# Edge ranks of a graph layer on one core: two TensorE products instead of three, the third term added on GpSimd

## The reference, cut to what matters

```python
def _spmm(row, col, val, x):                     # 53125 edges, sorted by dst
    return jax.ops.segment_sum(val[:, None] * x[col], row, num_segments=3125)
xn = _layernorm(x, axis=-1)
h = _spmm(edge_row, edge_col, edge_val, xn)      # and again in each layer
...
q, k, v = xn @ wq.T, xn @ wk.T, xn @ wv.T        # k and v are layer-normed per head
kv = einsum('bhsd,bhse->bhde', k, v) / S
```

## Time and profile before

| what | us |
|---|---|
| median of 3 runs | 1109.56 |
| their range | 1108.05 to 1111.23 |
| the profiled execution | 1103.93 |
| its span, first to last instruction | 1102.2 |
| records of the 25 tiles, first `spread` to last `kept` | 15.69 to 196.22 |
| busy in the span: PE, DVE, ACT, POOL | 1057.2, 710.7, 327.0, 181.0 |

### The profile page before, as it was taken

How to read it: one execution, slowest core, us unless ns; L and a number is a source line. 1 busy time by engine, 2 the same in 40 slices (tenths; PEclk the granted TensorE clock), 3 DMA queues, 4 the chain that set the end, 5 groups by cost and what they waited for, 6 DMA issues and landing times.

```text
span 1102.2 us, 15231 instructions
## 1 busy us (share of the span) xinstructions
PE 1057.2 (96%) x5391; PEld 662.0 (60%) x5391; DVE 710.7 (64%) x1611; ACT 327.0 (30%) x1067; POOL 181.0 (16%) x218
## 2 busy tenths in 40 slices
PE   4899999999999999999999999999999899999995
PEld 3566666566665665656784444644459466666664
DVE  8999999997766866869840111227777554444444
ACT  4878888312222222222211111211112221212210
POOL 2123444301101010110000000000444611111111
PEclk9999999999999999999999999999999999999998
DMA  6120011123333333423259988897994686555510
GB/s 179 19 58 13 38 48 48 49 96 135 134 135 134 135 134 135 182 101 139 97 220 361 377 300 310 337 334 285 305 325 169 188 238 141 137 136 135 132 38 8
DMA packets 80986, 178.58 MB, mean 162 GB/s; under 512 B 35678, under 2 KB 64122, under 8 KB 68750
## 3 DMA queue, kind: packets, MB, share of 16 engines
q1 hardware_dynamic: 67592, 123.39, 34.9%
q10 hardware_dynamic: 9190, 46.12, 10.6%
q0 software_dynamic: 4128, 8.08, 2.1%
HBM read 116.23 MB, written 63.77 MB: 163 GB/s over the span
## 4 chain that ended last, share of the span: by engine, by line
PE 84%; DVE 10%; issue 2%; ACT 2%; DMA 1%; POOLq 0%; DVEq 0%; ACTq 0%
PE ps L1692 23%; PE ps L1846 20%; PE ps L1971 10%; PE ps L1959 10%; PE ps L1676 8%; PE ps L1651 2%; PE ps L1715 2%; PE ps L1637 2%; PE ps L1671 1%; PE ps L1583 1%; PE ps L1658 1%; DVE W L1119 1%; DVE bst L1232 1%; DMA XX<-in_x 1%; DVE XT L1483 1%
## 5 line engine op out<-in xcount | busy, mean ns | idle before, releaser
L1692 PE MATMUL ps<-RING,XX 128*128 128x512 f32 (+2 forms) x700 | 296.1, 548 | 1.2 <-DVE W L1190 1.2
L1846 PE MATMUL ps<-RING,RY 128*128 128x512 f32 (+4 forms) x750 | 268.6, 514 | 0.1
L1846 PEld LDWEIGHTS ps<-RING,RY 128*128 128x128 f32 x750 | 133.5, 190 | 118.7 <-issue 111.2
L858 ACT COPY RING<-ps 128x512 f32<-128x512 f32 (+3 forms) x163 | 92.6, 568 | 274.9 <-PE ps L1676 258.9
L1692 PEld LDWEIGHTS ps<-RING,XX 128*128 128x128 f32 x700 | 117.5, 190 | 68.4 <-issue 61.6
L1183 DVE TENSOR_TENSOR RING<-RING,RY 128x1536 bf16<-128x1536 bf16 (+1 forms) x150 | 139.9, 939 | 4.0
L1676 PEld LDWEIGHTS ps<-RING 128*128 128x128 bf16 x1575 | 100.6, 97 | 52.0 <-issue 46.4
L1173 DVE TENSOR_TENSOR RING<-iota_p,RY 128x1024 bf16<-128x1024 bf16 (+1 forms) x150 | 96.3, 648 | 29.1 <-PE ps L1676 26.5
L1676 PE MATMUL ps<-RING 128*128 128x128 bf16 (+1 forms) x1575 | 112.9, 217 | 0.0
L995 ACT ACTIVATE RY<-ps,b1T 128x489 f32<-128x489 f32 x64 | 42.9, 671 | 164.8 <-PE ps L1959 164.8
L1550 DVE SCALAR_TENSOR_TENSOR W<-ps,RING,W 128x256 f32<-128x256 f32 (+1 forms) x32 | 15.4, 483 | 90.7 <-PE ps L1971 89.5
(11 more groups left out here) (287 smaller groups left out, 1332.6 us busy)
## 6 DMA issues: line engine op xcount, KB each, us to landing
RING<-adj_dram SPq DMA_DIRECT2D x60, 1280.0 KB, 7.0
adj_dram<-RING ACTq DMA_DIRECT2D x30, 1280.0 KB, 4.6
rbuf_dram<-W SPq DMA_DIRECT2D x8, 516.0 KB, 5.4
RING<-rbuf_dram SPq DMA_DIRECT2D x8, 516.0 KB, 4.0
xbuf_dram<-W SPq DMA_DIRECT2D x8, 512.0 KB, 3.3
XT<-in_L_ffn_w SPq DMA_DIRECT2D x16, 256.0 KB, 5.3
XT<-in_L_ffn_w SPq DMA_DIRECT2D x4, 1024.0 KB, 9.7
RING<-in_L_ffn_w SPq DMA_DIRECT2D x16, 256.0 KB, 5.0
```

Of the source, the lines that this page charges most:

```text
L858: nc.scalar.copy(RING[:, n % 2, at:at + w], ps[:, u % 2, 0:w]).then_inc(s_bev, 1)
L1692: last = nc.tensor.matmul(ps[:, ACC + dd, 0:w], XN[:, j, dd * H:(dd + 1) * H], at[:, i * w:(i + 1) * w], start=(j == 0), stop=True, skip_g ...
L1846: last = nc.tensor.matmul(o, (Y if l == 0 else S0)[:, j, :], RING[:, slot_of[g % 5], i * across + first:i * across + first + w], start=(j ...
```

## The change

- `ranks(j)` has two products in place of three. The first is as before; the second is the identity in fp16 times a new tile `tagged`.
- `tagged` (128 x 468, fp16, two buffers) is made by one addition on POOL: `ohp`, read back in the order of `scan`, plus `scan`. PE waits for it ahead of the second product (`s_tagged`).
- So that `ohp` carries the mark, `paired(j)` multiplies by 1024 while it copies; `kept(j)` multiplies by 1/1024 while it stores the records.
- On ACT `paired(it)` moves to the head of its round, ahead of `weigh(it - 3)`, `cast` and `normal`.
- On POOL the new addition stands first in the round (behind `pieces`, where there are any), then the two tiny adds, and the add of line 698 last.
- The 1024-times identity `own_b` goes; an fp16 identity `ident_h` comes in its place.

No DMA is added, removed or moved between queues.

```diff
+        tagged = [RY[:, 2000 + 234 * i:2234 + 234 * i].bitcast(F16) for i in range(2)]
...
-        own_b = sb("own_b", [P, P], BF16)
+        ident_h = sb("ident_h", [P, P], F16)
...
+        s_tagged = sem("s_tagged")
...
             for it in range(NT + KV_LAG + 1):
                 if it in CAST_AT:
                     pieces(CAST_AT[it])
-                if it > KV_LAG:
-                    m = it - KV_LAG - 1
-                    gp.wait_ge(s_khat, m + 1)
-                    ge(gp, s_vsum, m)
-                    gp.tensor_tensor(vacc.rearrange("p (c n) -> p c n", c=2), vacc.rearrange("p (c n) -> p c n", c=2), khat[m % 2][:, 2:4, 0:P], ALU.add).then_inc(s_vsum, 1)
+                if it < NT:
+                    gp.wait_ge(s_ohp, it + 1)
+                    ge(gp, s_rank, it - 1)
+                    gp.tensor_tensor(tagged[it % 2].rearrange("p (s c i) -> p s c i", c=C2, i=2), ohp[it % 2].rearrange("p (c s i) -> p s c i", s=NR, i=2),
+                                     scan[it % 2].rearrange("p (s c i) -> p s c i", c=C2, i=2), ALU.add).then_inc(s_tagged, 1)
                 if 1 <= it <= NT:
...
                     gp.tensor_tensor(whole, whole, w3, ALU.add).then_inc(s_wsum, 1)
+                if it > KV_LAG:
+                    m = it - KV_LAG - 1
...
-            nc.scalar.activation(own_b[:, :], ident[:, :], ACT.Copy, scale=OWN).then_inc(s_constb, 1)
+            nc.scalar.copy(ident_h[:, :], ident[:, :]).then_inc(s_constb, 1)
...
             def paired(j):
...
-                nc.scalar.copy(ohp[b].rearrange("p (c s i) -> p s c i", s=NR, i=2), ohs[b].rearrange("p (s c i) -> p s c i", c=C2, i=2)).then_inc(s_ohp, 1)
+                nc.scalar.activation(ohp[b].rearrange("p (c s i) -> p s c i", s=NR, i=2), ohs[b].rearrange("p (s c i) -> p s c i", c=C2, i=2), ACT.Copy, scale=OWN).then_inc(s_ohp, 1)

             def kept(j):
                 act.wait_ge(s_slotted, j + 1)
-                nc.scalar.copy(recs[:, j], ps[:, MISC, 0:140].rearrange("p (f g q) -> p g f q", f=5, q=4)).then_inc(s_recrd, 1)
+                nc.scalar.activation(recs[:, j], ps[:, MISC, 0:140].rearrange("p (f g q) -> p g f q", f=5, q=4), ACT.Copy, scale=1.0 / OWN).then_inc(s_recrd, 1)
...
                 u = it - BUILD_IT
+                if it < NT:
+                    paired(it)
                 if 0 <= u < LEAD:
                     weigh(u)
...
                 if it < NT:
-                    paired(it)
                     squares(it)
...
                 nc.tensor.matmul(o, before[:, :], sc[:, :, WC - 1:WC].to_broadcast([P, NR, WC]), start=True, stop=False)
-                nc.tensor.matmul(o, ident_b[:, :], scan[b], start=False, stop=False)
-                nc.tensor.matmul(o, own_b[:, :], ohs[b], start=False, stop=True).then_inc(s_rank, 1)
+                pe.wait_ge(s_tagged, j + 1)
+                nc.tensor.matmul(o, ident_h[:, :], tagged[b], start=False, stop=True).then_inc(s_rank, 1)
```

More of the change, by code:

```diff
@@ L706, in _ @@
                     gp.tensor_tensor(whole, whole, w3, ALU.add).then_inc(s_wsum, 1)
+                if it > KV_LAG:
+                    m = it - KV_LAG - 1
+                    gp.wait_ge(s_khat, m + 1)
+                    ge(gp, s_vsum, m)
+                    gp.tensor_tensor(vacc.rearrange("p (c n) -> p c n", c=2), vacc.rearrange("p (c n) -> p c n", c=2), khat[m % 2][:, 2:4, 0:P], ALU.add).then_inc(s_vsum, 1)
             gp.wait_ge(s_m, 1)
```

## The result

| what | before | after |
|---|---|---|
| median of 4 runs each, side by side, us | 1108.80 | 1127.36 |
| their range | 1107.79 to 1111.23 | 1125.51 to 1129.22 |
| the profiled execution | 1103.93 | 1129.22 |
| its span | 1102.2 | 1127.5 |

The ratio is 1.0161, with a 95% interval of 1.014 to 1.0182: 1.6% slower. Lines of the kernel after stand some lines lower in the file: 1102 is 1110, 1104 is 1112, 1111 is 1119, 1114 is 1122, 1119 is 1127, 1126 is 1134, 1142 is 1150, 1161 is 1169 (DVE); 824 is 831, 832 is 839, 836 is 843 (ACT); 698 is 713, 704 is 706, 706 is 708, and the new addition is 699 (POOL); 1624 is 1632, and the second product is 1634 (PE). In the experiments they shift by a few lines more; each view names its instruction.

The account below looks back on a forecast made before the run. PE and DVE were both taken as full, with DVE setting the pace: its round grows by 0.86 us to 7.26, over 23 rounds 19.8, less 2.4 of waits, +17.4; 1121.3 profiled, median 1127, range 1112 to 1147.

Parts of the forecast that it names:

- What bounds the kernel: In the records' rounds PE and DVE are both full: busy for 119.28 and 118.89 of 122.28 us.
- PE's product: One rank product fewer on PE saves 0.195 us a round, 4.9 over 25 rounds, but isn't seen; fp16 priced as bf16.
- ACT's scaled copies: On ACT they cost nothing: 0.30 us scaled, 0.29 plain; idle time covers the weights' delay of 0.62.
- The price of the addition: POOL's addition of 468 elements takes about 1.2 us and stalls DVE for 1.0, bounds 0.88 to 1.22.
- Where it falls: The addition misses DVE's line 1111 by 0.15 us, waits for line 1114, then holds line 1119 for 1.0; PE isn't late.
- POOL's new order: With line 698 behind the tiny adds, its stall of DVE goes from 0.49 to 0.35 us a round.
- DVE's wait for ACT's squares: Of DVE's 2.7 us of waits at line 1126 in the records, about 2.4 go.
- Three rounds with `pieces`: In rounds 1, 5 and 15 `pieces` precede the addition; 6.4 us, read in round 5, cover it and the rank product.
- The basis: The profiled execution's 1103.93 us becomes 1121.3; the median, 5.63 above it, becomes 1127.
- half price: POOL works two 16-bit elements at a time, so DVE's stall is 0.5 us: +5.9, 1115.5; chance 0.13.
- The faster one: The addition falls beside DVE's line 1111 and PE's saving shows: -3.1 us, 1106.4; chance 0.09.
- The ring: A loop over POOL's queue, PE and ACT takes 9.0 us a round: 1158, or 1143 in half the rounds; chance 0.12.

Follow-up runs that it names:

- experiments 1 to 3: Changed kernel with three products on PE, which doesn't wait for POOL's addition; addition made whole, by half, twice: 1126.83, 1119.57, 1150.07 us.
- experiment 10: Changed kernel without the addition, with three products and POOL's sum of the values back ahead of the tiny adds: 1117.21 us, ratio 1.0064.
- experiment 3: Changed kernel with three products and POOL's addition made twice a round, PE not waiting for it: 1150.07 us, ratio 1.0354.
- experiments 5 to 7: Changed kernel with POOL fills of 2.0, 1.1 and 0.5 us a round in place of the addition, PE waiting: 1133.52, 1121.83, 1115.07 us.
- experiment 4: Changed kernel with POOL's sum of the values put back ahead of the addition and the tiny adds: 1128.24 us, ratio 1.0149.
- experiment 5: Changed kernel with 2.0 us of POOL fills a round in place of the addition, PE waiting for them: 1133.52 us, ratio 1.021.
- experiment 9: Changed kernel without the addition and with three products, leaving only the new orders and scaled copies: 1113.47 us, ratio 1.0019.
- experiment 2: Changed kernel with three products and only half of POOL's addition (13 of 26 groups), PE not waiting for it: 1119.57 us, ratio 1.0069.

## Why the prediction was right

1127 was forecast, 1127.36 measured, and the +17.4 of the sum stands to the tenth at the product behind the records. The mechanism is the forecast one: DVE was full, and POOL's reading of SBUF takes time from it that PE's saving can't give back (experiments 1 to 3). That the figure fits to the tenth is partly luck; step by step:

- **What bounds the kernel**: borne out. DVE is as full as before, PE has 13.83 us of idle time in place of 3.00.
- **PE's product**: worth nothing, as forecast; fp16 goes at the pace of bf16 (0.37 beside 0.36).
- **ACT's scaled copies**: medians of 0.65 for `paired` (0.67 before) and 0.37 for `kept` (0.36). Their price is nothing; that of the new order is open (experiment 10).
- **The price of the addition**: the whole instruction was put at 1.2 and is 1.07 to 1.11 undisturbed; the stall was put at 1.0 and is 0.89, at the lower of the bounds. By the rule of the Trainium skill (SBUF — State Buffer, "Who interferes with whom"), the pair of ports is held for the whole instruction by whoever issued first, which with the measured 1.1 gives an estimate of 1.1 for the stall. The page words that rule for VectorE's two-port modes; of an instruction with two operands in SBUF it says that it contends with a GpSimd instruction that reads SBUF, and not for how long. The trace agrees with who keeps out whom, and with four fifths of the length: the fields' line shows 0.89.
- **Where it falls**: it misses the maximum, waits for line 1122 and holds up line 1127, as forecast. But it starts at 112.11 behind POOL's sum of the values, not when ACT's copy is there, and its result is late for PE. "In a round of the old length PE isn't late" failed: PE waited 20.5 us for it. This cost little, since DVE's maximum never waits for PE.
- **POOL's new order** was to give back 0.14 a round (0.49 now, 0.35 afterwards). DVE's busy time grew by 0.80 a round (133.21 less 118.89, over 18), of which 0.72 is the fields' line on the mean, 0.89 less the rounds in which the addition falls elsewhere. The other lines together took 0.08 instead of giving 0.14. So +1.00 and -0.14 were forecast, +0.72 and +0.08 came: two terms off in opposite directions. By the rounds it is 0.79 for 0.86.
- **DVE's wait for ACT's squares** The earlier trace rows was to shrink by 2.4; after, line 1134 has no wait in the list any more.
- **Three rounds with `pieces`**: the forecast was that 6.4 us cover the addition, without which PE would stand still for some 3 us. PE did stand still, 3.35 us until 60.23 in round 5 and 3.08 until 138.42 in round 15, and the granted clock fell behind both (0.50 from 60 to 64 us, 0.73 from 136 to 140). But DVE's maximum didn't wait, so the cover held where it counts: up to the end of the scan of tile 6 only 4.3 us are lost, about 5 rounds of 0.86.
- **The basis**: 1121.3 was the sum by the profiled execution, and the new one took 1129.2. The 7.9 between lie behind the records, in strips and experts. The step to the median took that in, because the execution shown of before was a quick one there.
- **The rivals**: half price is out (0.89, and experiment 3). The faster one is out: the addition is recorded with a median of 2.20 for 1.07 to 1.11 of work, so it waits for DVE in most rounds. The ring exists, but its 9.0 was mis-sized: the tiny adds and the sum of the values were put at 3.4, as they are when each waits for an instruction of DVE, and take 0.46 + 0.20 + 0.68 = 1.34 in the round shown, beside the scan and the maximum. With that the same sum gives 6.9, about DVE's round, and thus a limit of its own beside the ports (experiments 5 to 7) where the prediction had it bind far above DVE or not at all.

## What to carry to other kernels

Work moved to GpSimd isn't free because GpSimd is idle: here, where it reads SBUF, most of its time came out of VectorE's two-operand instructions, and a full VectorE lost 0.89 us to an addition that it does itself in 0.51. In a profile this loss stands as busy time, not as a wait, and the chain of waits may point at another loop of about the same length; compare each line's duration with its own in another trace. Open the loop in an experiment before believing the chain, and see in the new trace that it is open: in experiment 4 it wasn't. Before pricing a saving, look which other engine is as full as the one that is relieved.

## What the runs showed of the hardware that was not expected

- GpSimd's fills, of 2.0 us a round, left the two-operand instructions of VectorE that ran beside them at their length (0.69 and 1.13 us, experiment 5), while an addition of 1.1 us made one 0.89 longer.
- While one engine holds the operands, the one that waits goes next: with two additions one behind the other on GpSimd, the second is recorded from 114.84 with 2.23 us, for 1.07 to 1.11 of work, while VectorE's line 1134 runs until 116.12.
- Behind a wait of 2.4 us on TensorE the granted clock was 0.73, then 0.50 of full speed (experiment 10), behind one of 2.2 us 0.59 (the kernel before), and behind one of 1.8 us it stayed at 1.00 (experiment 9). The length of the wait doesn't settle it: behind one of 1.85 us it fell to 0.61 (experiment 2, 68 to 72 us), and behind one of 3.83 us it stayed at 1.00 (experiment 5, 60 to 72 us). What does isn't shown.
